# Layer 1 of a convolution-and-scan kernel: y copied one step earlier, Silu bursts inside bands, TensorE's small products first, the third step size summed one band step on

## The chip, the cores and the metric

The kernel runs on one core of a Trainium2 chip. Time is device time of one execution, in microseconds (us); of the kernel before there are three runs, and their median counts.

## What is computed

Two layers on x of 32 images, 96 channels, 56 x 56 pixels, all float32. Layer 0 is a depthwise 7x7 convolution, a layer norm over channels, two dense products with a gelu between, and a residual. Layer 1, where the change is, is a depthwise 5x5 convolution with Silu and a selective scan over the pixels (N = 4 states, R = 6):

```
x = silu(conv5x5(x) + conv_b);  xs = x.reshape(B, C, L)
dts, Bs, Cs = split(einsum('kd,bdl->bkl', x_proj_w, xs))
delta = softplus(einsum('dr,brl->bdl', dt_w, dts) + dt_b)
log_dA = maximum(delta * A, LOG_EPS)
P = exp(cumsum(log_dA));  dB_u = delta * Bs * xs
hs = P * cumsum(dB_u / maximum(P, EPS))
y = einsum('bdnl,bnl->bdl', hs, Cs) + xs * Ds
```

## The kernel before, in words

Layer 1 takes the images in 8 groups of 4. 4 images by 96 channels are three tiles of 128 rows, and the 3136 pixels are seven bands of 448. For each band, tile and state there is one **step**: 12 steps in a band (step j of a band: tile j // 4, state j % 4), S = 84 in a group. In what follows 5.3 is step 3 of band 5. Every engine runs its own list of instructions, in the order in which the code writes them, inside a loop over the groups, and they meet through semaphores alone. What the engines do in step s:

- VectorE (from line 1120): `gate` (line 1096, needs u of GpSimd), at some steps `sum_delta` (line 1070: the softplus's last sum, which gives the step size delta of one tile), `scan_q` for step s + 1 (line 1080, needs d_a of ScalarE), `scan_h` (line 1107), and two small copies.
- ScalarE (line 1223 on): `clip_a` and `exp_a` make d_a for step s + 5; `keep_front` copies transposed windows or convolution results out of PSUM (line 1151); `keep_b` and `keep_c` copy the rows of B and C (lines 1209, 1216); `keep_xd` copies the projection (lines 1166, 1168); `softplus` works on z in two parts (Abs and Exp, then Ln one step later, lines 1184, 1186, 1177); `keep_y` copies the finished y of a tile (line 1221); `silus` is a burst of Silu copies between two loads of an activation table (lines 1154 to 1160).
- GpSimd (line 1011 on): `times_c` multiplies h(s - 1) with a row of C, `times_b` makes u for step s + 3 (line 1000), and for the next band `split` (line 981, needs the copied projection) and `times_x` (line 988).
- TensorE (line 1388 on): `add_y` adds h(s - 2) to ps_y (line 1386), and at the first state of a tile starts ps_y with xs times D (line 1383), which needs the y before it copied; `spread_b` and `spread_c` (line 1356) put rows of B and C on all partitions through one bank, ps_bc, so that each waits for the copy of the one before; `project` (1335) and `delta_rows` (1349) prepare the next band.
- TensorE also makes the **front** of the next group, by the list `schedule`: 24 "turns" (15 small transposes of x, line 1306), 24 convolution units in two pieces of 12 products (line 1313), and 21 "backs" (4 transposes that bring a band of a tile into the scan's layout, line 1326), which stand in bursts, list `backs`, with ScalarE's Silus.
- SyncE issues all DMAs in one order: at its step s first the loads of slabs and taps for units that start by step s + 5 (line 915 waits until the unit three before has finished on TensorE), then, each fourth step, the store of y (line 932). There is one y buffer, and `keep_y` waits until its last store has landed.

The steps of the small work come from tables (lines 880 to 890). The bursts of before are at 0.0 (3 backs, of the group itself), 2.11 (3), 5.0 (7) and 6.0 (8); the last convolution piece is at 5.11.

## Time and profile before

| | us |
|---|---|
| runs of before | 4332.36, 4338.97, 4346.80 (median 4338.97) |
| the profiled execution | 4340.87 |
| its span | 4339.1 |
| mean granted clock of TensorE | 0.913 of full |

The profile is of one execution. A window's row says how long each engine was busy in a stretch; a group's row says how often an instruction stood, how long one took, and how long its engine had been idle just before such instructions, and behind the arrow what ended that idle time. Matmul records overlap where they are pipelined; there the time from the start of one to the start of the next is the cost.

### The profile page before, as it was taken

How to read it: one execution, taken by the hardware profiler on the slowest of the kernel's cores; microseconds unless marked ns; L12 is line 12 of the kernel's file. 1: busy time of each engine (PE TensorE's matmuls, PEld its weight loads, DVE VectorE, ACT ScalarE, POOL GpSimd, SP SyncE). 2: the span in 40 equal slices, each digit the busy share in tenths (PEclk: the TensorE clock that was granted, in tenths of full speed). 3: DMA queues.
4: the chain of work that ended last, by engine and by line, in shares of the span. 5: the costliest groups of instructions: out<-in, count | busy, mean ns of one | idle time of the engine just before them, and what ended most of it. 6: DMA issues, size and time to landing. Idle time of an engine off the chain costs nothing.

```text
span 4339.1 us, 74865 instructions
## 1 busy us (share of the span) xinstructions
PE 3840.0 (88%) x22806; PEld 2793.4 (64%) x22806; DVE 3258.9 (75%) x5219; ACT 2790.3 (64%) x4796; POOL 2263.5 (52%) x1928
## 2 busy tenths in 40 slices
PE   6999999999999999887888889888888888898877
PEld 6787878888787878675555545545545555455432
DVE  3767666676767675605988978879879889789899
ACT  1545455454636363657887877878778778778775
POOL 0323223232323242405776867767768677677787
PEclk9999999999999999987997988979979979889877
DMA  7565555556464644373423324424324334243100
GB/s 233 146 186 150 174 161 160 174 147 183 135 196 124 212 123 142 80 184 82 109 71 92 103 57 106 115 51 109 98 61 108 79 81 109 61 108 92 37 20 22
DMA packets 314879, 507.44 MB, mean 117 GB/s; under 512 B 190000, under 2 KB 255248, under 8 KB 314144
## 3 DMA queue, kind: packets, MB, share of 16 engines
q1 hardware_dynamic: 314432, 502.08, 42.3%
q8 instruction: 208, 3.41, 0.3%
q14 instruction: 239, 1.96, 0.2%
HBM read 424.94 MB, written 77.07 MB: 116 GB/s over the span
## 4 chain that ended last, share of the span: by engine, by line
PE 22%; DVE 12%; issue 9%; ACT 7%; POOL 5%; DMA 1%; DVEq 1%; ACTq 0%; POOLq 0%; SPq 0%
PE ps_front L1313 6%; PE ps_y L1386 5%; DVE ps_q L1080 5%; DVE h L1107 5%; PE ps_front L1306 3%; PE ps_prep L1335 2%; POOL u L1000 2%; PE ps_y L1383 2%; POOL h L1011 2%; PE ps_front L1326 1%; PE ps_bc L1356 1%; ACT d_a L1201 1%; DMA out_dram<-y 1%; ACT d_a L1195 1%; ACT y L1221 1%
## 5 line engine op out<-in xcount | busy, mean ns | idle before, releaser
L1011 POOL TENSOR_TENSOR h<-h,c_rows 128x448 f32<-128x448 f32 x672 | 766.7, 1141 | 366.1 <-DVE ps_q L1114 194.6
L522 ACT ACTIVATE act_h<-ps_up,b 128x448 f32<-128x448 f32 x672 | 408.9, 635 | 778.5 <-PE ps_up L640 778.3
L1000 POOL TENSOR_TENSOR u<-dxs,b_rows 128x448 f32<-128x448 f32 x672 | 767.0, 1141 | 48.0 <-ACT b_rows L1209 42.3
L1386 PE MATMUL ps_y<-h,ident 128*128 128x448 f32 x1344 | 733.2, 633 | 35.0 <-POOL h L1011 25.4
L319 POOL TENSOR_TENSOR h_low<-act_h,h_high 128x448 fp32r<-128x448 f32 x224 | 287.7, 1284 | 900.6 <-ACT h_high L527 900.6
L1080 DVE TENSOR_TENSOR_SCAN ps_q<-d_a,q_last,ps_q 128x448 f32<-128x448 f32 x576 | 659.6, 1145 | 13.2 <-ACT d_a L1201 13.2
L1107 DVE TENSOR_TENSOR_SCAN h<-d_a,ps_q 128x448 f32<-128x448 f32 x576 | 648.3, 1126 | 6.5 <-issue 6.2
L1313 PEld LDWEIGHTS ps_front<-win,taps 120*112 120x112 f32 x4608 | 538.4, 188 | 139.8 <-issue 136.4
L613 PE MATMUL ps_stage<-win,taps 124*112 124x112 f32 x6144 | 607.2, 260 | 2.7 <-DVE w_low L366 2.7
L613 PEld LDWEIGHTS ps_stage<-win,taps 124*112 124x112 f32 x6144 | 607.0, 178 | 3.3 <-DVE w_low L366 2.8
L1313 PE MATMUL ps_front<-win,taps 120*112 120x112 f32 x4608 | 550.8, 273 | 7.5 <-ACT win L1151 3.7
L1195 ACT ACTIVATE d_a<-delta,log_eps,a_neg 128x448 f32<-128x448 f32 x672 | 505.3, 752 | 46.8 <-DVE h L1107 28.5
L1096 DVE SCALAR_TENSOR_TENSOR ps_q<-ps_q,u 128x448 f32<-128x448 f32 x672 | 422.6, 629 | 120.6 <-POOL u L1000 115.2
L314 POOL TENSOR_TENSOR ln_rstd<-ln_var,minus_half 112x7 f32<-112x7 f32 x128 | 244.9, 1913 | 398.1 <-DVE ln_var L401 398.1
L429 DVE TENSOR_TENSOR conv<-ps_stage,bias_row 112x448 f32<-112x448 f32 x192 | 180.0, 937 | 349.4 <-PE ps_stage L613 349.4
L1386 PEld LDWEIGHTS ps_y<-h,ident 128*128 128x128 f32 x1344 | 250.7, 210 | 233.8 <-issue 158.1
L1201 ACT ACTIVATE d_a<-d_a 128x448 f32<-128x448 f32 x672 | 384.1, 572 | 2.7
L1383 PE MATMUL ps_y<-xs,skip 128*128 128x448 f32 x336 | 195.4, 668 | 194.9 <-ACT y L1221 194.6
L1070 DVE SCALAR_TENSOR_TENSOR delta<-ps_prep,z_log 128x448 f32<-128x448 f32 x168 | 103.7, 617 | 277.5 <-ACT z_log L1177 277.5
L1306 PEld LDWEIGHTS ps_front<-ident,x1pad 32*120 32x120 f32 x2880 | 212.7, 153 | 123.5 <-issue 121.8
L1151 ACT ACTIVATE conv<-ps_front 112x448 f32<-112x448 f32 x192 | 181.9, 947 | 170.4 <-PE ps_front L1313 170.3
L1151 ACT ACTIVATE win<-ps_front 120x480 f32<-120x480 f32 x192 | 204.2, 1065 | 127.3 <-PE ps_front L1306 125.1
(93 smaller groups left out, 7156.2 us busy)
## 6 DMA issues: line engine op xcount, KB each, us to landing
taps<-in_t_dram SPq DMA_DIRECT2D x192, 896.0 KB, 4.9
taps<-in_t_dram SPq DMA_DIRECT2D x192, 672.0 KB, 4.9
xres<-in_x_dram SPq DMA_DIRECT2D x224, 168.0 KB, 2.5
x_dram<-x1o SPq DMA_DIRECT2D x224, 168.0 KB, 2.0
x1pad<-x_dram SPq DMA_DIRECT2D x96, 392.0 KB, 8.1
out_dram<-y SPq DMA_DIRECT2D x168, 224.0 KB
xpad<-in_x_dram SPq DMA_DIRECT2D x29, 1176.0 KB, 10.4
conv<-in_x_dram SPq DMA_DIRECT2D x3, 1176.0 KB, 14.9
```

What stands on the lines that cost most here:

```text
L522: nc.scalar.activation(act_h[u % 2][:, t, :], ps_up[t][:, 0:BT], ACT.Gelu, bias=b1[:, t:t + 1]).then_inc(gelu_done, 1)
L613: mm = nc.tensor.matmul(ps_stage[q % 2][0:TOK, c * BLOCKS:(c + 1) * BLOCKS], taps[q % SLOTS1][0:WIN1, c, k, :], win[:, q * CQ + c, :, k:k ...
L1000: nc.gpsimd.tensor_tensor(u[s % U_SLOTS][:, :], dxs[:, t, :], b_rows[n][:, :], ALU.mult).then_inc(u_done, 1)
L1011: nc.gpsimd.tensor_tensor(h[s % H_SLOTS][:, :], h[s % H_SLOTS][:, :], c_rows[n][:, :], ALU.mult).then_inc(hc_done, 1)
L1080: nc.vector.tensor_tensor_scan(ps_q[s % 2][:, 0:BT], d_a[s % DA_SLOTS][:, :], no_q.broadcast_to([128, BT]), first, ALU.mult, ALU.add).then ...
L1096: nc.vector.scalar_tensor_tensor(ps_q[s % 2][:, 0:BT], ps_q[s % 2][:, 0:BT], 1.0, u[s % U_SLOTS][:, :], ALU.min, ALU.mult).then_inc(gated, 1)
L1107: nc.vector.tensor_tensor_scan(h[s % H_SLOTS][:, :], d_a[s % DA_SLOTS][:, :], ps_q[s % 2][:, 0:BT], first, ALU.mult, ALU.add).then_inc(h_d ...
L1151: nc.scalar.activation(dst, src, ACT.Copy).then_inc(front_kept, 1)
L1195: nc.scalar.activation(d_a[s % DA_SLOTS][:, :], delta[:, t, :], ACT.Relu, bias=log_eps[:, 0:1], scale=a_neg[:, t, n:n + 1]).then_inc(clipp ...
L1201: nc.scalar.activation(d_a[s % DA_SLOTS][:, :], d_a[s % DA_SLOTS][:, :], ACT.Exp, bias=LOG_EPS).then_inc(d_a_ready, 1)
L1313: mm = nc.tensor.matmul(bank[i][0:TOK, c * BLOCKS:(c + 1) * BLOCKS], taps[n % SLOTS2][0:WIN2, c, w, :], win[cb % 2][:, k * CQ + c, :, w:w ...
L1386: nc.tensor.matmul(ps_y[:, 0:BT], ident[:, :], h[s % H_SLOTS][:, :], start=False, stop=(n == N - 1)).then_inc(y_added, 1)
```

## The change

- y is copied by ScalarE in step 4r + 5 (r counts tiles) and no longer in 4r + 6, straight behind `clip_a`. SyncE's list of stores is as before.
- The turns start at step 1 and all of the front follows without a hole; three convolution units of the last channel block are done whole in one step. The last piece is at 5.9. The bursts stand at 0.0 (6 backs: bands 5 and 6 of the three tiles), 3.5 (3), 5.3 (7) and 5.10 (5).
- On TensorE the small products (projection, delta, B and C rows) stand ahead of a step's turn or convolution piece; at 0.0 and 5.10 ahead of the burst as well.
- The step sizes: products at steps 4, 5, 8 (before 3, 5, 7), Abs and Exp at 5, 6, 9 (before 4, 6, 8), sums at 8, 9 and, for the third tile, at step 0 of the band itself (before 7, 9, 11). GpSimd's `times_x` of that tile is at step 1 of the band.
- On ScalarE the copy of the projection, of y, and Ln go ahead of the rows of B and C and of `exp_a`; front copies after step 9 go behind all of these.

```diff
--- before.py
+++ after.py
@@ -821,10 +821,15 @@
         assert len(turns[0]) == CONVS
         units, schedule, backs = [], [[] for _ in range(S)], [[] for _ in range(S)]
 
-        def place(step, unit):
-            for piece in range(HALVES if unit[0] == "conv" else 1):
-                schedule[step + piece].append((len(units), piece))
+        def place(step, unit, at_once=False):
+
+            i, count = len(units), HALVES if unit[0] == "conv" else 1
             units.append(unit)
+            for piece in range(count):
+                schedule[step].append((i, piece))
+                if piece + 1 == count or not at_once:
+                    step += 1
+            return step
 
         def place_backs(step, runs):
             for t, b in runs:
@@ -832,25 +837,24 @@
                 units.append(("back", t, b, 0))
 
         for k in range(CONVS):
-            place(k, turns[0][k])
+            place(1 + k, turns[0][k])
+        step = CONVS + 1
         for cb in range(CBS):
             for k in range(CONVS):
-                if cb + 1 < CBS:
-                    step = CONVS + (cb * CONVS + k) * (HALVES + 1)
-                else:
-                    step = CONVS + cb * CONVS * (HALVES + 1) + k * HALVES
-                if step == 3 * STEPS - 1 + (STEPS - 1) % 2 - 1:
+                if cb + 1 == CBS and k == CONVS // 2:
+                    place_backs(step, [(0, 3), (0, 4)] + [(1, b) for b in range(5)])
+                last_cb = cb + 1 == CBS
+                step = place(step, ("conv", cb, k, 0), last_cb and k in (1, 3, 5))
+                if cb == 1 and k == 2:
                     place_backs(step, [(0, b) for b in range(3)])
-                if step == 5 * STEPS:
-                    place_backs(step, [(0, 3), (0, 4)] + [(1, b) for b in range(5)])
-                place(step, ("conv", cb, k, 0))
-                if cb + 1 < CBS:
-                    place(step + HALVES, turns[cb + 1][k])
-        place_backs(6 * STEPS, [(2, b) for b in range(6)] + [(0, 5), (1, 5)])
+                if not last_cb:
+                    step = place(step, turns[cb + 1][k])
+        assert step < 6 * STEPS
+        place_backs(step, [(2, b) for b in range(5)])
         EARLY = len(units)
-        place_backs(0, [(t, BANDS - 1) for t in range(TILES)])
+        place_backs(0, [(t, b) for b in (BANDS - 2, BANDS - 1) for t in range(TILES)])
         FRONT = len(units)
-        assert FRONT == CBS * (GI * TURNS2 + CONVS) + RUNS and max(len(pieces) for pieces in schedule) == 1
+        assert FRONT == CBS * (GI * TURNS2 + CONVS) + RUNS
         bank = [ps_front[(i + (i >= EARLY)) % 2] for i in range(FRONT)]
         unit_step = [None] * FRONT
         for step in range(S):
@@ -869,12 +873,12 @@
         PROJECT_AT = (0, 0, 1)
         XD_AT = 2
         SPLIT_AT = 3
-        DELTA_AT = (3, 5, 7)
-        Z_AT = (4, 6, 8)
-        SUM_AT = (7, 9, 11)
-        DXS_AT = (8, 10, 11)
-
-
+        DELTA_AT = (4, 5, 8)
+        Z_AT = (5, 6, 9)
+
+
+        SUM_AT, LAST_SUM_AT = (8, 9), 0
+        DXS_AT, LAST_DXS_AT = (9, 11), 1
         SPREAD_B_AT, KEEP_B_AT = (6, 7, 8, 9), (7, 8, 9, 10)
         SPREAD_C_AT, KEEP_C_AT = (10, 11), (11,)
         SPREAD_C_NOW, KEEP_C_NOW = {0: 2, 1: 3}, {0: 1, 1: 2, 2: 3}
@@ -983,7 +987,9 @@
 
             def times_x(f, b, t, first=False):
                 pool.wait_ge(delta_ready, f * RUNS + b * TILES + t + 1)
-                if not first:
+                if t + 1 == TILES:
+                    pool.wait_ge(u_done, (f * BANDS + b) * STEPS + 1)
+                elif not first:
                     pool.wait_ge(u_done, (f * BANDS + b - 1) * STEPS + (t + 1) * N)
                 nc.gpsimd.tensor_tensor(dxs[:, t, :], delta[:, t, :], xs[:, t, b * BT:(b + 1) * BT],
                                         ALU.mult).then_inc(dxs_ready, 1)
@@ -1021,19 +1027,19 @@
                         times_c(g, s - 1)
                     if prepare and j == SPLIT_AT:
                         split(f, fb)
-                    if prepare and j in DXS_AT[:-1]:
+                    if j == LAST_DXS_AT:
+                        times_x(g, b, TILES - 1)
+                    if prepare and j in DXS_AT:
                         times_x(f, fb, DXS_AT.index(j))
                     if s + U_AHEAD < S:
                         times_b(g, s + U_AHEAD)
                     elif more:
                         times_b(g + 1, s + U_AHEAD - S)
-                    if prepare and j == DXS_AT[-1]:
-                        times_x(f, fb, TILES - 1)
                 times_c(g, S - 1)
 
 
             split(0, 0, True)
-            for t in range(TILES):
+            for t in range(TILES - 1):
                 times_x(0, 0, t, True)
             for s in range(U_AHEAD):
                 times_b(0, s, True)
@@ -1064,7 +1070,9 @@
             def sum_delta(f, b, t, first=False):
                 n = f * RUNS + b * TILES + t + 1
                 dve.wait_ge(z_step, n * ZSTEPS)
-                if not first:
+                if t + 1 == TILES:
+                    dve.wait_ge(d_a_ready, (f * BANDS + b) * STEPS + 1)
+                elif not first:
                     dve.wait_ge(d_a_ready, (f * BANDS + b - 1) * STEPS + (t + 1) * N)
                     dve.wait_ge(dxs_ready, n - TILES)
                 nc.vector.scalar_tensor_tensor(delta[:, t, :], z_bank(t)[:, 0:BT], 0.0, z_log[t % Z_SLOTS][:, :],
@@ -1122,13 +1130,15 @@
                     if s > 0:
                         keep_h(g, s - 1)
                     gate(g, s)
+                    if j == LAST_SUM_AT:
+                        sum_delta(g, b, TILES - 1)
                     if (more or b + 1 < BANDS) and j in SUM_AT:
                         sum_delta(f, fb, SUM_AT.index(j))
                     if s + 1 < S:
                         scan_q(g, s + 1)
                     scan_h(g, s)
 
-            for t in range(TILES):
+            for t in range(TILES - 1):
                 sum_delta(0, 0, t, True)
             if last:
                 with dve.Fori(0, last) as g:
@@ -1225,28 +1235,31 @@
                     b, j = s // STEPS, s % STEPS
                     f, fb = next_band(g, b)
                     ahead = s + DA_SLOTS - 1
+                    prepare = more or b + 1 < BANDS
                     if more or ahead < S:
                         clip_a(g, ahead)
-                    if more:
+                    if s > N and (s - N - 1) % N == 0:
+                        keep_y(g, (s - N - 1) // N)
+                    if prepare and j == XD_AT:
+                        keep_xd(f, fb)
+                    if more and s <= CONVS + 1:
                         for i in kept_at[s]:
                             keep_front(g + 1, i)
-                    if s >= N + Y_LAG and (s - N - Y_LAG) % N == 0:
-                        keep_y(g, (s - N - Y_LAG) // N)
-                    if (more or b + 1 < BANDS) and j in KEEP_B_AT:
+                    if prepare and j - 1 in Z_AT:
+                        softplus(f, fb, Z_AT.index(j - 1), True)
+                    if prepare and j in KEEP_B_AT:
                         keep_b(f, fb, KEEP_B_AT.index(j))
-                    if (more or b + 1 < BANDS) and j in KEEP_C_AT:
+                    if prepare and j in KEEP_C_AT:
                         keep_c(f, fb, KEEP_C_AT.index(j))
                     if j in KEEP_C_NOW:
                         keep_c(g, b, KEEP_C_NOW[j])
                     if more or ahead < S:
                         exp_a(g, ahead)
-                    if more or b + 1 < BANDS:
-                        if j == XD_AT:
-                            keep_xd(f, fb)
-                        if j - 1 in Z_AT:
-                            softplus(f, fb, Z_AT.index(j - 1), True)
-                        if j in Z_AT:
-                            softplus(f, fb, Z_AT.index(j), False)
+                    if prepare and j in Z_AT:
+                        softplus(f, fb, Z_AT.index(j), False)
+                    if more and s > CONVS + 1:
+                        for i in kept_at[s]:
+                            keep_front(g + 1, i)
                     if s == 0:
                         silus(g, backs[0])
                     elif more and backs[s]:
@@ -1390,33 +1403,37 @@
                 for s in range(S):
                     b, j = s // STEPS, s % STEPS
                     f, fb = next_band(g, b)
-                    starts = [i for i, piece in schedule[s] if piece == 0] if more else []
-                    burst = backs[s] if more or s == 0 else []
-                    if not burst:
-                        for i in starts:
-                            front_waits(g + 1, i)
+                    prepare = more or b + 1 < BANDS
+                    burst = backs[s] if more or s == 0 else ()
+                    starts = [i for i, piece in schedule[s] if piece == 0] if more else ()
+                    early = [i for i in starts if units[i][0] == "turn"] if not burst else ()
+                    for i in early:
+                        front_waits(g + 1, i)
                     if s >= Y_LAG:
                         add_y(g, s - Y_LAG)
-                    if burst:
+                    if burst and starts:
                         for i in burst:
-                            back(g if s == 0 else g + 1, i)
-                        for i in starts:
+                            back(g + 1, i)
+                    for i in starts:
+                        if i not in early:
                             front_waits(g + 1, i)
                     if j in SPREAD_C_NOW:
                         spread_c(g, b, SPREAD_C_NOW[j])
+                    for t in range(TILES):
+                        if prepare and j == PROJECT_AT[t]:
+                            project(f, fb, t)
+                    if prepare and j in DELTA_AT:
+                        delta_rows(f, fb, DELTA_AT.index(j))
+                    if prepare and j in SPREAD_B_AT:
+                        spread_b(f, fb, SPREAD_B_AT.index(j))
+                    if prepare and j in SPREAD_C_AT:
+                        spread_c(f, fb, SPREAD_C_AT.index(j))
+                    if burst and not starts:
+                        for i in burst:
+                            back(g if s == 0 else g + 1, i)
                     if more:
                         for i, piece in schedule[s]:
                             front(i, piece)
-                    if more or b + 1 < BANDS:
-                        for t in range(TILES):
-                            if j == PROJECT_AT[t]:
-                                project(f, fb, t)
-                        if j in DELTA_AT:
-                            delta_rows(f, fb, DELTA_AT.index(j))
-                    if (more or b + 1 < BANDS) and j in SPREAD_B_AT:
-                        spread_b(f, fb, SPREAD_B_AT.index(j))
-                    if (more or b + 1 < BANDS) and j in SPREAD_C_AT:
-                        spread_c(f, fb, SPREAD_C_AT.index(j))
                 for s in range(S - Y_LAG, S):
                     add_y(g, s)
```

The places where it moves instructions. **TensorE, the first rows of the group loop.** (ps_bc with sel: a row of C; ps_prep with xproj: the projection; ps_front with conv2: backs; with x1pad: a turn.) Before:

```order
L1326 MATMUL ps_front1<-ident2,conv2 128x112 [waits front_kept]
L1326 MATMUL ps_front1<-ident2,conv2 128x112 x3
L1326 MATMUL ps_front0<-ident2,conv2 128x112 [waits front_kept]
L1326 MATMUL ps_front0<-ident2,conv2 128x112 x3
L1297 REGISTER_ALU
L1326 MATMUL ps_front1<-ident2,conv2 128x112 [waits front_kept]
L1326 MATMUL ps_front1<-ident2,conv2 128x112 x3
L1289 ISA
L1297 ISA [waits slab_ready0]
L1374 ISA [waits front_kept]
L1356 MATMUL ps_bc<-parts,sel 128x448 [waits c_kept]
L1306 MATMUL ps_front0<-ident2,x1pad 120x32 x15
```

and now:

```order
L1369 MATMUL ps_bc<-parts,sel 128x448 [waits c_kept]
L1345 ISA
L1347 ISA [waits front_kept]
L1348 MATMUL ps_prep0<-xs,xproj 128x448 [waits delta_ready]
L1345 REGISTER_ALU
L1348 MATMUL ps_prep0<-xs,xproj 128x448 [waits front_kept]
L1310 REGISTER_ALU
L1339 MATMUL ps_front0<-ident2,conv2 128x112 [waits front_kept]
L1339 MATMUL ps_front0<-ident2,conv2 128x112 x3
L1339 MATMUL ps_front1<-ident2,conv2 128x112 [waits front_kept]
L1339 MATMUL ps_front1<-ident2,conv2 128x112 x3
```

The row of C and the projections of two tiles, which stood behind the burst, are ahead of it. Six backs follow where three did, and no turn stands in this step.

**SyncE, the last loads of taps and the stores around them (5.0 on).** Before:

```order
L915 DMA taps2_0<-in_t2_dram 128x1344 [waits front_done]
L912 REGISTER_ALU
L915 DMA taps2_1<-in_t2_dram 128x1344 [waits front_done]
L931 REGISTER_ALU
L932 ISA [waits y_kept]
L932 DMA out_dram<-y 4x32x448
L912 REGISTER_ALU
L915 DMA taps2_2<-in_t2_dram 128x1344 [waits front_done]
L931 REGISTER_ALU
L932 ISA [waits y_kept]
L932 DMA out_dram<-y 4x32x448
```

and now:

```order
L919 DMA taps2_0<-in_t2_dram 128x1344 [waits front_done]
L916 REGISTER_ALU
L919 DMA taps2_1<-in_t2_dram 128x1344 [waits front_done]
L916 REGISTER_ALU
L919 DMA taps2_2<-in_t2_dram 128x1344 [waits front_done]
L935 REGISTER_ALU
L936 ISA [waits y_kept]
L936 DMA out_dram<-y 4x32x448
```

The first store here is that of tile run r = 14. It stood behind two loads of taps, and the third load came after it; now all three loads are ahead of it.

**ScalarE, band 0.** Before, the end of step 0.4 and step 0.5 (z_log with ps_prep: Abs; z_log from z_log: Exp, and in 0.5 Ln; win2: a copied turn):

```order
L1200 REGISTER_ALU
L1201 ACTIVATE d_a3<-d_a3 128x448 [waits clipped]
L1179 REGISTER_ALU
L1184 ACTIVATE z_log0<-ps_prep1 128x448 [waits delta_ready,z_done]
L1185 ISA
L1186 ACTIVATE z_log0<-z_log0 128x448 [waits z_step]
L1195 ACTIVATE d_a4<-delta,log_eps,a_neg 128x448 [waits h_done]
L1143 REGISTER_ALU
L1151 ACTIVATE win2_0<-ps_front0 120x15x32 [waits front_done]
L1200 REGISTER_ALU
L1201 ACTIVATE d_a4<-d_a4 128x448 [waits clipped]
L1176 REGISTER_ALU
L1177 ACTIVATE z_log0<-z_log0 128x448 [waits z_step]
```

and now, step 0.5:

```order
L1205 ACTIVATE d_a4<-delta,log_eps,a_neg 128x448 [waits h_done]
L1230 ISA [waits y_added]
L1231 ACTIVATE y<-ps_y 128x448 [waits y_stored]
L1153 REGISTER_ALU
L1161 ACTIVATE win2_0<-ps_front1 120x15x32 [waits front_done]
L1210 REGISTER_ALU
L1211 ACTIVATE d_a4<-d_a4 128x448 [waits clipped]
L1189 REGISTER_ALU
L1194 ACTIVATE z_log0<-ps_prep1 128x448 [waits delta_ready,z_done]
L1195 ISA
L1196 ACTIVATE z_log0<-z_log0 128x448 [waits z_step]
```

The copy of y, which stood in step 0.6, is now in 0.5, ahead of the band's first Abs and Exp; these stood in 0.4, and have moved one step on.

## Rows read from the trace of the kernel before

**Rows 1.** The page's first part, busy time and share of each engine.
```profile
PE 3840.0 (88%) x22806; PEld 2793.4 (64%) x22806; DVE 3258.9 (75%) x5219; ACT 2790.3 (64%) x4796; POOL 2263.5 (52%) x1928
```

**Rows 2.** Windows, the seven bands of the group from 2887.5: stretch, length, engines, clock, DMA.
```profile
2887.50:2939.30 51.80, 45.64 (x214) 28.09 (x214) 36.85 (x64) 36.33 (x58) 30.28 (x28) 0.60 0.29 67
2939.30:2976.80 37.50, 34.17 (x212) 22.57 (x210) 36.69 (x64) 31.81 (x55) 30.73 (x29) 1.00 0.48 121
2976.80:3015.00 38.20, 34.47 (x207) 22.91 (x206) 36.84 (x65) 30.63 (x55) 31.26 (x29) 0.96 0.44 109
3015.00:3056.80 41.80, 35.80 (x225) 23.75 (x225) 36.67 (x65) 36.34 (x61) 30.91 (x29) 1.00 0.43 108
3056.80:3093.40 36.60, 32.84 (x200) 21.93 (x199) 36.53 (x64) 30.28 (x54) 30.74 (x29) 1.00 0.39 115
3093.40:3143.80 50.40, 43.16 (x223) 30.28 (x222) 36.91 (x64) 36.12 (x62) 30.93 (x29) 0.86 0.40 95
3143.80:3187.90 44.10, 34.46 (x101) 16.05 (x100) 33.71 (x42) 33.77 (x60) 31.72 (x29) 0.86 0.07 20
```

**Rows 3.** Timeline, VectorE, two successive gates of an undisturbed stretch: start, length.
```profile
2523.57 0.63 DVE L1096 SCALAR_TENSOR_TENSOR ps_q<-ps_q,u 128x448 f32<-128x448 f32 x1
2526.49 0.63 DVE L1096 SCALAR_TENSOR_TENSOR ps_q<-ps_q,u 128x448 f32<-128x448 f32 x1
```

**Rows 4.** Groups of instructions of that group of images: busy, mean ns, idle before them.
```profile
L1096 DVE SCALAR_TENSOR_TENSOR ps_q<-ps_q,u 128x448 f32<-128x448 f32 x84 | 52.8, 629 | 16.8 <-POOL u L1000 16.0 <-issue 0.4
L1070 DVE SCALAR_TENSOR_TENSOR delta<-ps_prep,z_log 128x448 f32<-128x448 f32 x21 | 13.0, 618 | 22.0 <-ACT z_log L1177 22.0
L1383 PE MATMUL ps_y<-xs,skip 128*128 128x448 f32 x42 | 23.3, 639 | 22.8 <-ACT y L1221 22.8
L1011 POOL TENSOR_TENSOR h<-h,c_rows 128x448 f32<-128x448 f32 x84 | 96.1, 1144 | 48.9 <-ACT c_rows L1216 25.0 <-DVE ps_q L1114 23.1 <-DVE h L1107 0.7
L981 POOL TENSOR_TENSOR parts<-xd,high 128x448 fp32r<-128x448 f32 x7 | 8.0, 1138 | 27.8 <-ACT high L1168 27.8
```

**Rows 5.** Timeline, TensorE, band 0 of the group from 2587.6.
```profile
2589.24 1.75 PE L1326 MATMUL ps_front<-ident,conv 112*128 112x112 f32 x8 [3.06 <-issue]
2600.57 1.86 PE L1335 MATMUL ps_prep<-xs,xproj 128*128 128x448 f32 x2
2602.22 1.70 PE L1383 MATMUL ps_y<-xs,skip 128*128 128x448 f32 x2
2608.86 1.69 PE L1386 MATMUL ps_y<-h,ident 128*128 128x448 f32 x2
2610.48 1.71 PE L1306 MATMUL ps_front<-ident,x1pad 32*120 32x32 f32 x15
2612.12 1.86 PE L1386 MATMUL ps_y<-h,ident 128*128 128x448 f32 x2
```

**Rows 6.** Windows, a stretch of the same band 0.
```profile
2608.70:2632.40 23.70, 23.11 (x92) 13.68 (x91) 13.95 (x26) 15.65 (x26) 16.10 (x15) 0.50 0.35 86
```

**Rows 7.** Timelines of ScalarE, then GpSimd, then VectorE, the same band 0.
```profile
2590.07 0.53 ACT L1216 ACTIVATE c_rows<-ps_bc 128x448 f32<-128x448 f32 x1
2591.08 1.28 ACT L1154 ACT_TABLE_LOAD   x1
2596.05 0.76 ACT L1195 ACTIVATE d_a<-delta,log_eps,a_neg 128x448 f32<-128x448 f32 x1
...
2603.87 1.13 POOL L981 TENSOR_TENSOR parts<-xd,high 128x448 fp32r<-128x448 f32 x1 [4.44 <-ACT high L1168]
...
2606.19 0.63 DVE L1096 SCALAR_TENSOR_TENSOR ps_q<-ps_q,u 128x448 f32<-128x448 f32 x1 [2.69 <-POOL u L1000]
```

**Rows 8.** Timeline of TensorE, then chain of waits, then timeline of ScalarE, band 5.
```profile
3096.38 0.93 PE L1326 MATMUL ps_front<-ident,conv 112*128 112x112 f32 x8
...
3117.64 6.90 DMA out_dram<-y
...
3124.56 0.54 ACT L1221 ACTIVATE y<-ps_y 128x448 f32<-128x448 f32 x1 [1.91 <-DMA out_dram<-y]
```

## Prediction

> **What bounds the kernel now.** The page comes first: TensorE is busy for 88% of the span and no engine for more [rows 1], but that is a mean over two layers. So I cut one group of layer 1 into its bands with the windows view [rows 2]. VectorE is busy for about 36.7 us in each of bands 0 to 5, and band 4 lasts 36.6: there VectorE runs without a hole, one step in 2.92 us [rows 3]. That is the floor, and 33.7 us of VectorE in band 6. Above it lie 15.2 us in band 0, 0.9, 1.6 and 5.2 in bands 1 to 3, 13.8 in band 5 and 10.4 in band 6, 47 us of a group's 300.4. Only these can be won, and anything that moves must not add to them.
>
> The groups of instructions say what VectorE waits for: 22.0 us ahead of sum_delta for ScalarE's Ln, 16.0 us ahead of the gate for GpSimd's u [rows 4]. GpSimd is late since it stands for 25.0 us before a copied row of C and for 27.8 us before the copied projection [rows 4]. Both come late behind the Silu bursts at the start of bands 0, 5 and 6. TensorE stands 22.8 us a group, 21 times, for the copy of y [rows 4]; with its busy time of 33 to 34 us in bands 1, 2 and 4 [rows 2] it is nearly as full as VectorE there.
>
> **Bursts out of the band's start (bands 2, 3, 5, 6).** At 3.5 and 5.3 the rows of C and the projection of the band are copied already, so GpSimd's waits behind those two bursts go. Band 2 loses the burst at 2.11: -1.5 (none to -1.6). Band 3 gets it at 3.5, where ScalarE's burst of some 4.6 us lies just ahead of the Ln that the sum at 3.8 wants; I count 1.2 of its 5.2 us as left: -4 (0 to -5.2). Band 6 loses the burst of 8 at its start, but the 5 backs at 5.10 end about 6 us before the first row of C is wanted at best, and TensorE arrives late there; u is made three steps ahead (7.8 us), which takes most of it. I count 5 of 10.4 us left: -5 (0 to -9).
>
> **Band 0.** Its burst has 6 backs now, and they stand behind a row of C and two projections. In the old order TensorE started the burst at 2589.24 [rows 5]. Now it first waits for the C row that ScalarE copies at 2590.07 to 2590.60 [rows 7]. From there clip and the C copy (1.2), C's next row (0.7), the third projection (1.65), its two copies (1.2) and parts to 2608.7, u to 2609.8: the gate that stood at 2606.19 [rows 7] stands at 2609.9, **+3.7**.
>
> TensorE's step 0.2 begins at 2608.0 instead of 2602.22. A step of half clock with a turn costs 1.62 for the addition and 1.64 for the turn (2608.86, 2610.48, 2612.12, [rows 5]), 3.3 us against VectorE's 2.92, and more where a start of y (1.6), a delta product (1.1) or a row of B (0.65) comes on top. Steps 2 to 8 make 4.9 + 3.3 + 4.4 + 4.4 + 5.5 + 3.9 + 5.0 = 31.4: 2639.4. The y copy of step 0.9 now waits for the addition of that same step (2641.0), and the Abs and Exp of the third tile stand behind it; with a window copy, a B row, exp, clip and Ln that is 4.9 more: 2645.9 to the third sum, and the first step of band 1 comes at 2647.7, 60.1 us after the first of band 0. Rows 2 show 51.8: **+8.3** (3 to 12: the lower end if the waits for y, 3 times about 1.1, and the gap before the burst are all won back, the upper if a half-clock stretch of three steps more follows). TensorE enters band 1 some 9 us behind, of which VectorE bears about 6 without a stall: band 1 +1.4 (0 to +3).
>
> **The y copy.** One step earlier, it frees TensorE from most of 22.8 us [rows 4] where TensorE leads. Where TensorE is behind, ScalarE now waits for the addition, and the copy of C (at j = 1) or B (at j = 9) behind it makes TensorE wait in turn, about 1 us each. So I take the gain in bands 1 to 4 as spent on TensorE's lag, with +1 for band 4 (0 to +3), where 10 convolution pieces stand for 8.
>
> **Band 5.** What is late next is the store of y. In the order the store of r = 14 now has three loads of taps ahead, and the last waits for the unit done at 5.4, behind the burst of 7. From the burst's start (the old one: 3096.38, [rows 8]) to that unit's end I work out 12.1: 6.7 for the burst, 2.5 for a piece at half clock, 0.9 + 0.6 + 1.4 for the rest. 0.6 for issuing and 6.90 for landing [rows 8] make 19.6; y, exp, Abs, Exp, the front copy, clip and Ln 3.9: the first sum can stand 23.5 us after the burst began. VectorE wants it 13.5 us after the first scan of that step, and TensorE begins the burst 3 to 7 us after that scan, since it is behind (3096.38 against a step that began at 3093.4, [rows 2, 8]). So 13 to 17 us of stall take the place of 13.8 us: **+3** (-9 if the loads have drained by then, +8 at worst). The Trainium skill, "DMA: Bandwidth & Descriptors", Anatomy of one DMA, puts a transfer's fixed part at about 2 us, mostly the write receipt. By that the store would land nearly 5 us sooner and the estimate for the kernel would be some 34 us lower; the trace has 6.90 here, and the row is what I use.
>
> **No change of time:** the products ahead of the pieces only reorder TensorE's own list; they bring z and B rows 1.3 us (2.5 at half clock) sooner, which is in the terms above. The third sum one band step on has three steps before its first use by clip_a. The last group has no front: 3 more backs, +4; ahead of the loop 3 backs, a sum and a product less, -4.
>
> **Sum.** 8.3 + 1.4 - 1.5 - 4 + 1 + 3 - 5 = +3.2 us a group, times the seven groups that carry a front: +22. The profiled execution took 4340.87, so **4363 us**; the median of the runs shown is 1.9 lower, which changes nothing. About 0.3% (13 us) is what a measurement of this kernel can tell from no change.
>
> **Rivals.**
> *Faster: TensorE's freed time decides.* The 22.8 us are won where TensorE is full, its lag stays below 6 us, and the store lands in time. Then bands 1 to 3 lose their 7.7 us, band 5 loses 6 and band 6 loses 6 beside band 0's +8.3: -11.4 a group, 4261. For it: TensorE's waits are all for y in bands 1, 2 and 4, and 41 us of ScalarE-borne waits [rows 4] hang on bursts that move. Against it: band 5's store. It decides if the y copy of 5.5 is not held by the DMA. 0.34.
> *The clock opens in band 0.* TensorE was busy 23.11 of 23.7 us there and stayed at 0.50, its lower level [rows 6]; much of that work is turns. Now a C row and two projections stand together without transposes. If that opens the clock for the backs and part of the turns, band 0 costs no more than before: -5.1 a group, 4305. The Trainium skill, "TensorE: Matmul & The Clock Gate", Part 4, says that transposes do not count as a busy engine; by that, band 0 stays at the lower level until the first convolution, and by its Part 1 a busy engine would be at the higher. 0.06.
> *The gains and losses cancel:* band 5 comes out level and band 6 wins 6 to 8; the moves of order then do in time nothing that can be seen, 4341. 0.14.
> *Much slower: the stores pile up.* The copies at 4.9, 5.1 and 5.5 are each held by a store behind loads, from the point where TensorE enters band 4 more than 6 us behind. Each costs 3 to 4 us: +10 a group, 4411. 0.06.
> The forecast's own case has 0.40.
>
> **Numbers.** Slower 0.40 + 0.06 = 0.46, within 0.3% 0.14, faster 0.34 + 0.06 = 0.40. The forecast's own range is 4355 to 4390; both signs hold much of the chance, so the range for 8 in 10 goes from 4250 (just under the faster case) to 4415.
>
> **What would show it.** Windows by band of the profile after: band 0 near 60 us, bands 2, 3 and 4 within 38, band 5 near 53, band 6 near 39. Idle before the y start (22.8) under 10; GpSimd's waits for C rows and projection (52.8 together) halved, and most of what is left in band 0. In band 5 ScalarE's y copy released by the DMA. If band 0 lasts 55 us or less, or the y copy of 5.5 is not released by the store, the forecast is wrong and the kernel faster; a first sum of band 4 that waits over 3 us would point to the last rival.

## The result, and the profile after

| | us |
|---|---|
| kernel before, 4 runs | 4342.08 (4332.36 to 4346.80) |
| changed kernel, 4 runs | 4624.27 (4621.09 to 4626.23) |
| ratio | 1.0652, 95% interval 1.0632 to 1.0673 |
| profiled execution, span | 4619.3, mean granted clock 0.88 |

The change makes the kernel 282 us slower. The forecast was +22.

The windows view of the changed kernel, the seven bands of the group from 3346.7, cut where VectorE starts the first `scan_h` of each band (stretch, length, busy time of PE, PEld, DVE, ACT, POOL, clock, DMA share, GB/s; it answers to [rows 2]):

```profile
3346.70:3397.97 51.27, 39.18 (x196) 24.21 (x197) 36.97 (x65) 36.38 (x59) 30.97 (x28) 0.68 0.33 77
3397.97:3439.45 41.48, 36.47 (x218) 23.30 (x217) 36.81 (x64) 30.78 (x55) 30.99 (x28) 0.98 0.42 103
3439.45:3478.94 39.49, 32.45 (x193) 21.50 (x193) 36.80 (x64) 30.26 (x54) 30.96 (x28) 0.90 0.42 109
3478.94:3529.94 51.00, 44.95 (x227) 28.52 (x226) 36.84 (x64) 35.38 (x59) 30.77 (x29) 0.81 0.33 84
3529.94:3572.94 43.00, 32.51 (x200) 21.91 (x201) 36.80 (x64) 30.61 (x54) 31.26 (x29) 0.93 0.25 78
3572.94:3636.96 64.02, 53.33 (x267) 35.61 (x266) 36.80 (x64) 37.05 (x63) 30.97 (x29) 0.83 0.37 88
3636.96:3683.43 46.47, 37.35 (x77) 15.79 (x77) 34.05 (x41) 31.67 (x57) 30.82 (x28) 0.71 0.06 17
```

The group takes 336.7 us, 36.3 more than in [rows 2], and VectorE's own work is unchanged. Groups differ a little from each other, so the bands are also given as means over six groups (the second to the seventh), in us:

| band | 0 | 1 | 2 | 3 | 4 | 5 | 6 |
|---|---|---|---|---|---|---|---|
| before | 51.7 | 37.5 | 38.1 | 41.8 | 36.7 | 50.1 | 43.1 |
| changed | 53.9 | 42.3 | 40.0 | 50.8 | 43.3 | 63.2 | 44.6 |
| difference | +2.2 | +4.8 | +1.9 | +9.0 | +6.6 | +13.1 | +1.5 |
| forecast | +8.3 | +1.4 | -1.5 | -4 | +1 | +3 | -5 |

That is 39 us a group. No single stall does it: the undisturbed bands 1 and 4 lost their even run as well.

The groups view of that group of images says who waits (busy, mean ns, idle before; it answers to [rows 4], and adds ps_bc, where TensorE spreads a row of B or C, and ScalarE's copies):

```profile
L1078 DVE SCALAR_TENSOR_TENSOR delta<-ps_prep,z_log 128x448 f32<-128x448 f32 x21 | 13.1, 622 | 54.0 <-ACT z_log L1187 53.8 <-issue 0.2
L1104 DVE SCALAR_TENSOR_TENSOR ps_q<-ps_q,u 128x448 f32<-128x448 f32 x84 | 52.9, 630 | 14.7 <-POOL u L1006 13.9 <-issue 0.4
L1231 ACT ACTIVATE y<-ps_y 128x448 f32<-128x448 f32 x21 | 11.4, 544 | 66.2 <-PE ps_y L1399 48.6 <-DMA out_dram<-y 17.6
L1369 PE MATMUL ps_bc<-parts,sel 32*128 32x448 f32 x56 | 31.2, 556 | 49.3 <-ACT b_rows L1219 19.3 <-ACT c_rows L1226 19.0 <-ACT win L1161 10.8
L1396 PE MATMUL ps_y<-xs,skip 128*128 128x448 f32 x42 | 27.7, 750 | 4.9 <-ACT y L1231 4.4 <-ACT win L1161 0.6
L1017 POOL TENSOR_TENSOR h<-h,c_rows 128x448 f32<-128x448 f32 x84 | 95.9, 1142 | 87.2 <-DVE ps_q L1122 44.0 <-ACT c_rows L1226 40.1 <-DVE h L1115 3.0
L985 POOL TENSOR_TENSOR parts<-xd,high 128x448 fp32r<-128x448 f32 x7 | 8.0, 1138 | 13.9 <-ACT high L1178 13.9
```

And the same view of the kernel before, the three rows of it that [rows 4] leave out:

```profile
L1221 ACT ACTIVATE y<-ps_y 128x448 f32<-128x448 f32 x22 | 12.3, 560 | 15.1 <-PE ps_y L1386 13.2 <-DMA out_dram<-y 1.9
L1356 PE MATMUL ps_bc<-parts,sel 32*128 32x448 f32 x56 | 28.0, 500 | 1.1 <-ACT b_rows L1209 0.6 <-ACT c_rows L1216 0.5
L1151 ACT ACTIVATE conv<-ps_front 112x448 f32<-112x448 f32 x24 | 22.8, 949 | 17.8 <-PE ps_front L1313 17.7
```

VectorE pays at the sums: 54.0 us ahead of `sum_delta`, 22.0 before, 32 of the 36. Two waits are new behind that. ScalarE stands 66.2 us a group at the y copy (15.1 before), and TensorE stands 49.3 us ahead of ps_bc (1.1 before): 38.3 for copies of B and C rows and 10.8 for a front copy (win). The 22.8 us that TensorE waited for y have shrunk to 4.9 as planned. The two engines wait for each other: ScalarE for the addition, TensorE for copies that stand behind the y copy in ScalarE's list.

One such meeting, in timelines of TensorE, ScalarE and VectorE, band 1 of the changed kernel (start, length, in brackets idle before):

```profile
3417.22 0.71 PE L1362 MATMUL ps_prep<-parts,dtw_high 128*128 128x448 f32 x1
3417.77 0.37 PE L1362 MATMUL ps_prep<-parts,dtw_low 128*128 128x448 f32 x1
3417.98 1.34 PE L1326 MATMUL ps_front<-win,taps 120*112 120x112 f32 x12
3419.16 0.93 PE L1399 MATMUL ps_y<-h,ident 128*128 128x448 f32 x2
...
3417.19 0.75 ACT L1205 ACTIVATE d_a<-delta,log_eps,a_neg 128x448 f32<-128x448 f32 x1
3420.20 0.54 ACT L1231 ACTIVATE y<-ps_y 128x448 f32<-128x448 f32 x1 [2.27 <-PE ps_y L1399]
...
3423.51 0.56 ACT L1187 ACTIVATE z_log<-z_log 128x448 f32<-128x448 f32 x1
...
3424.26 0.62 DVE L1078 SCALAR_TENSOR_TENSOR delta<-ps_prep,z_log 128x448 f32<-128x448 f32 x1 [2.94 <-ACT z_log L1187]
```

The clock is full here. In TensorE's list a product, a convolution piece and then the addition stand in a row; ScalarE's y copy, second in its step, waits 2.27 us for the end of that row. The rest of its step and the next step's Ln stand behind it, and VectorE stands 2.94 us for that Ln ahead of its sum.

### The profile page after: what moved, and what is told of

It is laid out like the page before. It is cut to its first block, busy times and chain, and to the rows that moved or that the text cites. A ratio compares the mean times of both kernels' runs of the same rounds, so it can differ in the third digit from the quotient of the medians.

```text
span 4619.3 us, 74818 instructions
## 1 busy us (share of the span) xinstructions
PE 3965.5 (86%) x22806; PEld 2843.2 (62%) x22806; DVE 3265.3 (71%) x5219; ACT 2768.1 (60%) x4796; POOL 2264.6 (49%) x1928
## 4 chain that ended last, share of the span: by engine, by line
PE 30%; ACT 9%; issue 7%; DVE 5%; POOL 4%; DMA 3%; ACTq 1%; DVEq 0%; SPq 0%; POOLq 0%
PE ps_front L1326 8%; PE ps_y L1399 8%; PE ps_prep L1348 3%; PE ps_bc L1369 3%; DMA out_dram<-y 3%; PE ps_front L1319 3%; DVE ps_q L1088 2%; DVE h L1115 2%; POOL u L1006 2%; PE ps_y L1396 2%; POOL h L1017 2%; PE ps_front L1339 1%; ACT d_a L1205 1%; ACT b_rows L1219 1%; ACT d_a L1211 1%
## 5 line engine op out<-in xcount | busy, mean ns | idle before, releaser
L1399 PE MATMUL ps_y<-h,ident 128*128 128x448 f32 x1344 | 768.3, 663 | 27.9 <-POOL h L1017 26.6
L1326 PE MATMUL ps_front<-win,taps 120*112 120x112 f32 x4608 | 581.8, 282 | 5.3 <-ACT win L1161 3.7
L1369 PE MATMUL ps_bc<-parts,sel 32*128 32x448 f32 x448 | 248.8, 555 | 377.6 <-ACT b_rows L1219 167.7
L1369 PEld LDWEIGHTS ps_bc<-parts,sel 32*128 32x128 f32 x448 | 96.8, 216 | 732.1 <-ACT b_rows L1219 273.0
L1231 ACT ACTIVATE y<-ps_y 128x448 f32<-128x448 f32 x168 | 91.4, 544 | 523.1 <-PE ps_y L1399 394.3
L1399 PEld LDWEIGHTS ps_y<-h,ident 128*128 128x128 f32 x1344 | 263.5, 225 | 190.4 <-issue 129.9
L636 PE MATMUL ps_up<-hn_high,w_high 96*128 96x448 f32 x672 | 254.4, 379 | 34.6 <-DVE hn_low L411 19.8
```

What stands on the lines that cost most here:

```text
L1326: mm = nc.tensor.matmul(bank[i][0:TOK, c * BLOCKS:(c + 1) * BLOCKS], taps[n % SLOTS2][0:WIN2, c, w, :], win[cb % 2][:, k * CQ + c, :, w:w ...
L1369: return nc.tensor.matmul(ps_bc[:, 0:BT], sel[rows, which, :], parts[rows, :], start=True, stop=True)
L1399: nc.tensor.matmul(ps_y[:, 0:BT], ident[:, :], h[s % H_SLOTS][:, :], start=False, stop=(n == N - 1)).then_inc(y_added, 1)
```

## The experiments

Each ratio is to the kernel before run beside it; a per cent is about 43 us. "Group" times are means over six groups, from the starts of VectorE's scans. "Small products" are those of rows, projection and delta. "Store first" puts the store of y into SyncE's step 4r + 6, one step sooner, and ahead of that step's loads.

| run | time, us | ratio |
|---|---|---|
| e1 change, y copy back in 4r+6 | 4385.93 | 1.0109 (1.0088 to 1.0129) |
| e2 change, small products back behind the piece | 4552.05 | 1.0484 (1.0462 to 1.0506) |
| e3 both of these back | 4395.29 | 1.0128 (1.0100 to 1.0155) |
| e4 change, store first | 4524.05 | 1.0408 (1.0364 to 1.0452) |
| e8 change, y copy last in ScalarE's step 4r+5 | 4366.40 | 1.0059 (1.0032 to 1.0085) |
| e10 change, third sum and tables back | 4563.37 | 1.0525 (1.0482 to 1.0567) |
| e11 change, front copies early in the step | 4699.23 | 1.0843 (1.0797 to 1.0890) |
| e14 change, old schedule and bursts | 4471.28 | 1.0299 (1.0274 to 1.0324) |
| e5 before, new y copy | 4309.50 | 0.9925 (0.9899 to 0.9951) |
| e6 before, store first | 4290.51 | 0.9874 (0.9844 to 0.9904) |
| e7 before, third sum and tables | 4375.42 | 1.0082 (1.0055 to 1.0109) |
| e9 before, e5 and e7 together | 4416.15 | 1.0191 (1.0154 to 1.0227) |
| e12 before, new schedule and bursts | 4397.61 | 1.0133 (1.0097 to 1.0169) |
| e13 before, e5 and e12 together | 4429.80 | 1.0200 (1.0176 to 1.0225) |
| e15 before, new y copy and store first | 4278.16 | 0.9854 (0.9832 to 0.9876) |
| e16 e15 and small products first | 4553.52 | 1.0494 (1.0467 to 1.0520) |
| e17 e6 and small products first | 4599.44 | 1.0596 (1.0572 to 1.0620) |
| e18 e15 and Ln, projection copies early | 4291.76 | 0.9889 (0.9867 to 0.9911) |

### The y copy and the products' order, taken back (e1 to e3)

```diff
-                    if s > N and (s - N - 1) % N == 0:
-                        keep_y(g, (s - N - 1) // N)
+                    if s >= N + Y_LAG and (s - N - Y_LAG) % N == 0:
+                        keep_y(g, (s - N - Y_LAG) // N)
```

That is e1, in ScalarE's list at the same place of its step. e2 writes TensorE's `front(i, piece)` ahead of `project`, `delta_rows` and the spreads, except at the bursts; e3 does both.

> The changed kernel with the copy of y back in step 4r+6 (all else as changed). Theory 1 (the y copy ties ScalarE to TensorE's addition of the same step and to the store): of the 40 us a group that the change costs, the 66 us of idle before the y copy fall to about 15 and the sum at step 8 waits under 20 us instead of 54; the kernel takes 4400 to 4480 us. Theory 2 (the products ahead of the pieces make TensorE wait for the row copies, 49 us a group): little comes back, 4570 to 4630 us, and the 49 us stay.

> The changed kernel with the turn or convolution piece again ahead of a step's small products on TensorE (the products stay ahead of the bursts at 0.0 and 5.10, and of the turn at 3.5). Theory 1 (y copy): 4560 to 4630 us, y waits unchanged. Theory 2 (order of products): TensorE's idle before the rows of B and C falls from 49 us a group to under 10, and the kernel takes 4400 to 4480 us.

> Both of these undone; what stays are the burst positions, the third sum one band on, the tables and ScalarE's order. If the two parts explain the loss, 4290 to 4360 us, at or below the kernel before. Rival (the bursts and band 0 cost): 4400 or more, with band 0 at 54 us or more and band 5 over 55 us.

e1 gives back 238 of 282 us, more than its range allowed. e2 gives back 72; its 4552 lies in neither of the two ranges, so each theory had a part. But beside the old y copy the order is worth nothing (e1 against e3: -9 us, within the intervals). Both keep 47 to 56 us of loss. So the loss looked like the y copy's, and later runs show that this was only half of it.

### The store's place (e4, e6)

```diff
+                    if s >= N + Y_LAG and (s - N - Y_LAG) % N == 0:
+                        store(g, (s - N - Y_LAG) // N)
                     while todo and unit_step[todo[0][2]] <= s + AHEAD:
                         load, k, _ = todo.pop(0)
                         load(g + 1, False, k)
-                    if s >= N + Y_LAG + 1 and (s - N - Y_LAG - 1) % N == 0:
-                        store(g, (s - N - Y_LAG - 1) // N)
```

> The changed kernel with SyncE's store of y at its step 4r+6 and ahead of that step's loads, so that no load of taps stands between a y copy and its store. If the store queue decides (my prediction's band 5): the 17.6 us a group that the y copy waits for the DMA go to under 3, band 5 falls from 63 to about 52 us, and the kernel takes 4480 to 4540 us. Rival (ScalarE waits for TensorE's addition, 48.6 us a group): the wait only changes its name, 4590 to 4625 us.

> The kernel before, with SyncE's store of y issued in step 4r+6 and ahead of that step's tap loads. In the kernel before only 1.9 us a group was waited for the store (ScalarE's y copy, band 5). Theory that the store's place behind loads costs only where the copy comes early: within 0.3% of the kernel before, 4325 to 4345. If loads that now stand behind the store's wait come late: above 4352.

In the changed kernel the DMA holds ScalarE for 17.6 us a group. Timelines of SyncE's queue, of ScalarE and of TensorE, band 4:

```profile
3539.48 0.58 SPq L936 DMA_DIRECT2D out_dram<-y  x1
3542.38 17.82 SPq L919 DMA_DIRECT2D taps<-in_t_dram  x3
3560.45 0.58 SPq L936 DMA_DIRECT2D out_dram<-y  x1
...
3566.80 0.54 ACT L1231 ACTIVATE y<-ps_y 128x448 f32<-128x448 f32 x1 [5.44 <-DMA out_dram<-y]
3567.24 0.54 ACT L1219 ACTIVATE b_rows<-ps_bc 128x448 f32<-128x448 f32 x1
...
3569.19 1.04 ACT L1161 ACTIVATE win<-ps_front 120x480 f32<-120x480 f32 x1
...
3570.36 0.73 PE L1369 MATMUL ps_bc<-parts,sel 32*128 32x448 f32 x1 [7.15 <-ACT win L1161]
```

The same store in the chain of waits (start, length to landing):

```profile
3560.45 6.33 DMA out_dram<-y
```

The store stands behind three loads of taps, and the last of these waits for a unit of TensorE. It goes out at 3560.45 and lands after 6.33 us, and the next y copy is 5.44 us late. Behind it in ScalarE's step stand the row of B and, last, the copy of a turn (win). TensorE waits for that one: ahead of its small products it has the wait for the windows of the next convolution. It is idle for 7.15 us and comes back at the lower clock (granted 0.50 from 3570.3 to 3576; a spread takes 0.73 us, against 0.46 at full clock). With the store first the DMA wait is gone (the y copy's 59.0 us of waiting are all TensorE's now), band 5 falls from 63.2 to 51.3 us, and the kernel is 100 us faster. In the kernel before it is worth 50 us, where I had expected nothing: band 5 falls from 50.1 to 45.5 us and band 0 from 51.7 to 47.2, while band 6 takes 1.4 more (the wait at `sum_delta` falls from 22.0 to 13.2 us in e6). Only in band 5 did its y copy wait for the store (1.9 us). In band 0 it is the clock that differs: in six of the seven groups the granted clock of its first 17 us is 0.65 to 0.70 in e6 and 0.50 to 0.51 in the kernel before. How the store's place brings that about no run shows.

### The parts alone and in pairs (e5, e7, e9, e12, e13, e10, e14)

```diff
+                    if s > N and (s - N - 1) % N == 0:
+                        keep_y(g, (s - N - 1) // N)
                     if more:
                         for i in kept_at[s]:
                             keep_front(g + 1, i)
-                    if s >= N + Y_LAG and (s - N - Y_LAG) % N == 0:
-                        keep_y(g, (s - N - Y_LAG) // N)
```

That is e5, on the kernel before. e7 takes the change's tables and its VectorE and GpSimd parts:

```diff
-        DELTA_AT = (3, 5, 7)
-        Z_AT = (4, 6, 8)
-        SUM_AT = (7, 9, 11)
-        DXS_AT = (8, 10, 11)
+        DELTA_AT = (4, 5, 8)
+        Z_AT = (5, 6, 9)
+        SUM_AT, LAST_SUM_AT = (8, 9), 0
+        DXS_AT, LAST_DXS_AT = (9, 11), 1
```

e12 the change's `place` and its units (with the small products ahead of the turn at the bursts alone); e9 and e13 add e5 to these (e13 with a convolution piece's wait behind the addition, as in the change). e10 and e14 undo the same parts in the changed kernel (e14 with the bursts behind the small products of their step, but for the one at 0.0).

> The kernel before, with the y copy alone moved to step 4r+5, behind clip_a. If the early copy does harm by itself (it ties ScalarE to TensorE's addition of that step, and the addition stands behind the piece of the step before, and waits for the store of the last y), this costs about as much as it does inside the change: 150 to 240 us, 4500 to 4580. If it does harm only because the small products now stand ahead of the pieces or because of the bursts' new places, it costs under 60 us here (4340 to 4400).

> The kernel before, with only the third step size's sum, product and the tables DELTA, Z, SUM and DXS as in the change (third sum in step 0 of the band). With the change's other parts undone, the rest of the change (e1, +47 us) was left open between this part and the bursts. If the third sum is at fault: 4370 to 4420. If the bursts are: within 15 us of the kernel before or faster.

> The kernel before, with only the convolution's new schedule: one step later, bursts of transposes at steps 0.0, 3.5, 5.3 and 5.10 (at those the small products ahead of the turn, as in the changed kernel). If the rest of e1 (+47 us) is due to the third sum alone (e7: +36 us), this is within 15 us of the kernel before. If the bursts cost by themselves, by ScalarE's row of copies in front of a logarithm: 4370 to 4420, with the wait at step 8 of band 5 or at its sums.

> The kernel before with two parts together: the y copy in step 4r+5 (alone 0.9925 of the kernel before) and the third sum with its tables (alone 1.0082). If the parts add, 4307 to 4330. Theory of the meeting: with the tables' new places the first sum of a band (step 8) needs a logarithm of ScalarE's step 6 that stands behind the y copy of step 5, and the product of step 4 stands ahead of the addition that this copy waits for, so together they cost far more than the parts: above 4420, with the wait in front of the sum of step 8.

> The kernel before with the y copy in step 4r+5 and the convolution's new schedule (one step later, bursts moved), a piece of the convolution waiting for its copies behind the addition as in the changed kernel. Alone these gave 0.9925 and 1.0133; if they add, 4360 to 4380. Theory that the early copy's harm comes from its meeting with the shifted schedule (e10 left 218 us without the third sum): 4480 or more. If the harm needs ScalarE's new order within the step as well, or the small products' order: 4380 to 4450.

> The changed kernel with the third sum and the tables DELTA, Z, SUM, DXS as in the kernel before; the y copy stays in step 4r+5. Theory of the meeting: most of the 282 us goes, under 4450. If the y copy's cost inside the change comes from the copies of finished pieces that now stand at the end of ScalarE's step, little changes: above 4550.

> The changed kernel with the convolution's old schedule (pieces a step earlier, bursts at 0.0, 2.11, 5.0 and 6.0), the y copy still in step 4r+5. Theory of the meeting with the shifted schedule: under 4480. If the harm is in ScalarE's order and the products' order: above 4550.

The y copy alone is a gain, 0.75%, where its expectation had no gain. The gain lies in band 0 (47.8 against 51.7 us; the granted clock from 17 to 38 us into the band is 0.69 to 0.89, against 0.54 to 0.58) and in band 6 (40.4 against 43.1); the full bands 1 and 4 take 1.1 and 1.7 us more. The third sum costs 0.8% and the bursts 1.3%. With the y copy each costs more than its parts: 0.9925 and 1.0082 would make 1.0007, and e9 has 1.0191 (about 80 us more); 0.9925 and 1.0133 would make 1.0058, and e13 has 1.0200 (some 60 us more, with the moved wait of e13 in it). From the other end, undoing the third sum gives back 1.3% and undoing the schedule 3.5%. So the theory that the y copy's harm is its meeting with the third sum's tables does not hold: e9 fell just short of its 4420, and e10 stands at 4563 where it said under 4450. The meeting with the schedule has a larger part (e14 gives back 153 us), but by itself it doesn't make the harm either: e13 was to reach 4480 for that and has 4430. Schedule and bursts alone (e12) cost 6.2 us in band 1 (43.7 against 37.5), 6.0 in band 3 and 3.5 in band 5, and give back 5.6 in band 0.

### Where ScalarE's step waits (e8, e11)

```diff
-                    if s > N and (s - N - 1) % N == 0:
-                        keep_y(g, (s - N - 1) // N)
...
                     elif more and backs[s]:
                         silus(g + 1, backs[s])
+                    if s > N and (s - N - 1) % N == 0:
+                        keep_y(g, (s - N - 1) // N)
```

That is e8, on the changed kernel. e11, on the changed kernel, puts the copies of finished pieces (win, conv, xs) behind the y copy, near the start of the step:

```diff
-                    if more and s <= CONVS + 1:
+                    if more:
                         for i in kept_at[s]:
                             keep_front(g + 1, i)
...
-                    if more and s > CONVS + 1:
-                        for i in kept_at[s]:
-                            keep_front(g + 1, i)
```

> The changed kernel, with the y copy in step 4r+5 but as ScalarE's last work of the step instead of its second. Theory that ScalarE's rows for the next products stand behind a y copy that waits for TensorE: with only the next step's clip_a behind it, most of the 48.6 us a group of waiting goes, 4390 to 4450. Theory that the copy comes too early whatever stands behind it (store, addition): above 4500.

> The changed kernel with ScalarE's copies of finished pieces (win, conv, xs) back near the step's beginning, behind the y copy, in all steps. Theory that TensorE's next piece is held by the late copy, and the addition and the y copy behind that piece: under 4500. Theory of the meeting of y copy and third sum's tables: above 4580.

e8 has the same copy in the same step, but with nothing of its step behind it, and gives back 258 of 282 us. It is a near neighbour of e1: in ScalarE's list the two differ only in whether the copy stands ahead of the next step's `clip_a` or behind it. So the two runs agree that what counts is the work of step 4r + 5 that stands behind the copy; the number of the step does not. The groups view of e8:

```profile
L1231 ACT ACTIVATE y<-ps_y 128x448 f32<-128x448 f32 x21 | 11.6, 551 | 30.4 <-PE ps_y L1399 18.2 <-DMA out_dram<-y 12.3
L1369 PE MATMUL ps_bc<-parts,sel 32*128 32x448 f32 x56 | 27.6, 493 | 19.9 <-ACT c_rows L1226 9.8 <-ACT b_rows L1219 6.9 <-ACT win L1161 3.0
L1078 DVE SCALAR_TENSOR_TENSOR delta<-ps_prep,z_log 128x448 f32<-128x448 f32 x21 | 13.0, 617 | 25.5 <-ACT z_log L1187 25.2 <-issue 0.2
```

ScalarE still waits 30.4 us for y, but TensorE's wait for rows falls from 49.3 to 19.9 and VectorE's at the sums from 54.0 to 25.5. So the number that speaks is the wait of the work behind, not that of the copy. e11 speaks against the other theory, that the late front copies are what costs, by holding TensorE's pieces and with them the y copy: moved early, they take TensorE's wait for win away, but the kernel is 75 us slower still. One more copy early in the step now waits for TensorE (32.2 us a group ahead of conv, and TensorE 54.3 at ps_bc).

### The products' order in the kernel before (e15 to e18)

```diff
                     if j in SPREAD_C_NOW:
                         spread_c(g, b, SPREAD_C_NOW[j])
-                    if more:
-                        for i, piece in schedule[s]:
-                            front(i, piece)
...
                     if (more or b + 1 < BANDS) and j in SPREAD_C_AT:
                         spread_c(f, fb, SPREAD_C_AT.index(j))
+                    if more:
+                        for i, piece in schedule[s]:
+                            front(i, piece)
```

That is the edit that e16 and e17 share. e15 joins e5 and e6, and e18 moves two things of ScalarE's step in e15:

```diff
+                    if more or b + 1 < BANDS:
+                        if j == XD_AT:
+                            keep_xd(f, fb)
+                        if j - 1 in Z_AT:
+                            softplus(f, fb, Z_AT.index(j - 1), True)
                     if (more or b + 1 < BANDS) and j in KEEP_B_AT:
```

> The kernel before with the y copy in step 4r+5 (alone 0.9925) and the store in 4r+6 ahead of the tap loads (alone 0.9874). If both take away the same wait of band 5: like the store alone, 0.985 to 0.989. If they add, since a copy that comes early leans more on the store: 0.975 to 0.983, about 4250.

> e15 and, on TensorE, the small products ahead of the convolution's piece. In the changed kernel with the old y copy this order was worth 9 us (4386 against 4395). If that holds here: 5 to 15 us below e15. If the products' waits for ScalarE's rows hold the piece, and the addition of the next step behind it, up in front of the early y copy: 30 us or more above e15.

> e16 without its early y copy: the kernel before with the store in 4r+6 ahead of the loads (4290 alone) and the small products ahead of the convolution's piece. Theory that the products' order harms only together with the early y copy: within 1% of 4290 (4250 to 4335). If this order is harmful by itself in the kernel before: above 4400, and e16 says nothing of the early copy.

> e15 (4278) with, within ScalarE's step, the copies of high and xd and the softplus' logarithm ahead of the row copies and the exponential, as in the changed kernel. If a sum waits for its logarithm behind these: 10 to 30 us below e15. If the decay of the next step, which then comes 0.6 us later, is what DVE waits for: 0 to 30 us above.

With e6 these make a two by two table, all with the store first: neither 4290, y copy 4278, order 4599, both 4554. The order alone costs 309 us, the largest single effect of all. The early y copy does no harm beside it; it gains some 45 us there, against some 10 without, where the two intervals overlap. Of the two theories for e17 mine was the wrong one, and so was the reading of e1 and e3, that the order is harmless: it is so inside the change and not in the kernel before. One difference between the two is that the front copies stand late in ScalarE's step in the change and early in the kernel before, and the groups view of e17 has the wait in front of them:

```profile
L1151 ACT ACTIVATE conv<-ps_front 112x448 f32<-112x448 f32 x24 | 22.7, 948 | 55.4 <-PE ps_front L1313 55.4
L1151 ACT ACTIVATE win<-ps_front 120x480 f32<-120x480 f32 x24 | 25.4, 1056 | 26.9 <-PE ps_front L1306 26.9
L1221 ACT ACTIVATE y<-ps_y 128x448 f32<-128x448 f32 x21 | 11.7, 558 | 4.7 <-PE ps_y L1386 4.7
```

17.8 us ahead of conv became 55.4. ScalarE's own wait for y is small, but everything that ScalarE copies is late: TensorE stands 30.0 us for the copied y (22.8 before), and VectorE 29.1 us ahead of the gate (16.8) and 31.6 ahead of the sums (22.0). The timelines of TensorE and ScalarE in e17 show one turn of the wheel:

```profile
3402.68 0.47 PE L1356 MATMUL ps_bc<-parts,sel 32*128 32x448 f32 x1
3403.08 1.77 PE L1335 MATMUL ps_prep<-xs,xproj 128*128 128x448 f32 x4
3404.68 1.34 PE L1313 MATMUL ps_front<-win,taps 120*112 120x112 f32 x12
3405.86 0.93 PE L1386 MATMUL ps_y<-h,ident 128*128 128x448 f32 x2
3407.42 0.46 PE L1356 MATMUL ps_bc<-parts,sel 32*128 32x448 f32 x1 [0.63 <-ACT c_rows L1216]
...
3402.01 0.75 ACT L1195 ACTIVATE d_a<-delta,log_eps,a_neg 128x448 f32<-128x448 f32 x1
3406.06 0.93 ACT L1151 ACTIVATE conv<-ps_front 112x448 f32<-112x448 f32 x1 [3.31 <-PE ps_front L1313]
3406.80 0.56 ACT L1216 ACTIVATE c_rows<-ps_bc 128x448 f32<-128x448 f32 x1
```

The row of C was ready in PSUM at 3403.15. ScalarE stands 3.31 us for the conv piece, which TensorE does last, and copies the row at 3406.80; TensorE, done with its addition at 3406.79, waits for it at 3407.42. ScalarE waits for TensorE's last work of a step, TensorE for a row behind that wait.

## Why the prediction was wrong

**The direction came from the wrong account.** The only large loss in the forecast's sum was band 0, and that term failed: +8.3 forecast, +2.2 measured. Part of it is the clock. Windows of the same part of band 0 (from some 17 us into it): the changed kernel in this group, the kernel before, and e12, the kernel before with the new schedule and bursts alone:

```profile
3364.00:3385.00 21.00, 16.91 (x117) 10.63 (x116) 11.33 (x19) 16.97 (x28) 14.97 (x14) 0.83 0.62 149
```

```profile
3205.00:3226.00 21.00, 20.41 (x100) 11.41 (x100) 10.22 (x18) 14.34 (x24) 16.39 (x15) 0.58 0.53 132
```

```profile
2928.60:2949.60 21.00, 17.64 (x130) 10.52 (x128) 13.43 (x23) 18.52 (x32) 16.96 (x16) 0.92 0.64 149
```

That is the rival "the clock opens in band 0", in three of the seven groups: there the granted clock of this part is 0.83 and the band takes 51.3 to 52.5 us. In the other four it is 0.50 to 0.58, and the band takes 53.6 to 55.8, still short of the 60.1 that was worked out. The rival's reason was not borne out: e12 has its burst ahead of the projections, as in the kernel before, and a clock of 0.74 to 0.92 there in all seven groups (band 0: 46.1 us). In the group shown TensorE worked without a hole from 3360.68 on, at 0.50 up to 3367, and had 1.00 from 3370 to 3382. The Trainium skill, "TensorE: Matmul & The Clock Gate", Part 4, says that transposes don't count as a busy engine. The prediction drew from it that band 0 stays at the lower level until the first convolution, and that did not hold: from 3370 to 3382 turns stand between additions and delta products, and no convolution had run yet.

**"The y copy."** This step failed. It said that the row copies behind the y copy "make TensorE wait in turn, about 1 us each", and that this is paid out of the 22.8 us; I took it at 0, with +1 for band 4. Measured inside the change (e1) it is 238 us, 34 a group, and in the kernel before (e5) -31. I had the wait right and its price wrong: I priced the wait of one copy and not what stands behind it. As I read the timelines, the y copy holds the rows and the late front copies, these hold the products, and with the products ahead of the piece they hold the addition for the next copy. The order alone doesn't close this circle: in the kernel before with that order the early copy gains some 45 us (e16 against e17).

**"No change of time: the products ahead of the pieces only reorder TensorE's own list."** The second failure. An order within one engine is free only if no other engine waits for its last item. Taking it back inside the change gives 72 us (e2), and bringing it into the kernel before, with the store first, costs 309 (e17).

**Bands 1 to 4.** Forecast +1.4, -1.5, -4 and +1; measured +4.8, +1.9, +9.0 and +6.6. In band 3 the burst at 3.5 was counted as a gain. With the old y copy band 3 still takes 45.8 us (e1), and with schedule and bursts alone 47.8 (e12), against 41.8: the new schedule with its burst costs 4 to 6 us there.

**Band 5.** The mechanism (the store behind three loads of taps, the last of which waits for TensorE) was right, and so was the landing of 6.90 us (6.36 for the store of 5.5, issued at 3608.99, for which the y copy waits 6.70 us). The size was not: +13.1, beyond the +8 given as worst. (The 13 to 17 us worked out in place of 13.8 make -1 to +3; the sum took the upper end.) e4 takes 11.9 of the 63.2 us away by the store's place. The rival in which stores pile up had the right place (bands 4 and 5) and, at +10 us a group, nearly the price that e4 shows (100 us, 14 a group); it had a chance of 0.06, and it was not the larger part of the loss.

**Band 6** came out at +1.5 (forecast -5). **The last group** was forecast at +4 and measured at +3.6, and what stands ahead of the loop at -4 and measured at +3.5. With 273 us for the seven groups that carry a front these make the 280 us between the two profiled spans.

**The named checks.** The idle time ahead of the y start fell to 4.9 (under 10, right). GpSimd's wait for the projection halved (27.8 to 13.9, right), that for rows of C rose from 25.0 to 40.1 (wrong): those rows now stand behind the y copy in ScalarE's list. Bands 2 to 4 within 38 us was wrong in all three, and so were band 5 near 53 (63.2) and band 6 near 39 (44.6). The y copy of 5.5 is released by the DMA (right). Band 0 took less than 55 us, which was to mean a faster kernel, and the kernel was 282 us slower: this sign took the rest of the sum for granted. The first sum of band 4 waits 1.94 us in this group, under the 3 named as the sign of stores piling up, and yet they do: the chain of waits passes a store 21 times, three times a group, where it was 7 before.

**What is shown and what is not.** Shown by exchange are that the y copy ahead of the rest of step 4r + 5 costs 238 to 258 us inside the change (e1, e8), that the store's place is worth 100 us in the change and 50 before (e4, e6), and that the products' order costs 309 us in the kernel before (e17 against e6). That the waits form a loop is read from the groups and the timelines. No pair of parts makes a loss of 238 us in the kernel before: the early copy costs some 45 us beside the third sum (e9 against e7), some 30 beside the schedule (e13 against e12), and gains some 45 beside the order. Beside ScalarE's new order of the step it was tried only in part (e18). Why the order is harmless inside the change stays open too. The front copies' place is one difference between e17 and e1 or e3; others are the schedule, the third sum, the early Ln, and TensorE's wait for a convolution's windows, which stands ahead of the addition in e17 and behind it in the change. The direct test, e17 with the front copies at the end of ScalarE's step, was not run. Nor is it explained why e2, with the pieces first again, keeps 210 us of loss; e9 and e13 give 80 and 60 of it as meetings with the y copy.

**A better kernel.** The early y copy and the early store, with nothing else of the change, give 4278 (0.9854), 1.5% below the kernel before; the store alone gives 4290 (0.9874), and the two intervals overlap. Ln and the projection's copies early, tried on top (e18), gained nothing: 4292, with an interval that overlaps e15's.

## What to carry to other kernels

Where two engines copy for each other within one step, try an instruction that waits for the other engine's last work of a step at the end of one's own step, or a step later. Its price is not its own wait but the waits of the engine that it feeds: look at what stands behind it in its list and who waits for that. The parts of such a change can't be added up: try each alone and each taken back, since here a gain of 31 us became a loss of 238 beside the other parts. And a store that a single buffer depends on goes ahead of loads that wait for compute.

## What the hardware showed that I had not expected

A store of 224 KB took 6.1 to 7.3 us to land wherever the chain of waits of the two kernels passes one (6.33 at 3560.45), long after SyncE had issued it in 0.58. The Trainium skill, "DMA: Bandwidth & Descriptors", Anatomy of one DMA, has a fixed part of about 2 us, for transfers that GpSimd issues; these are SyncE's, and no run here separates the fixed part from the rest. TensorE came back at a granted clock of 0.50 after the single idle stretch of 7.15 us (0.73 us for a spread that takes 0.46), so that waits cost it twice: in the group above the matmuls that start y have a mean of 750 ns where the kernel before had 639 [rows 4], with the same number of them.
